# A first pass over an image batch: two rows a partition and one queue, against four rows, quarter tiles of the array and two queues

## The reference, cut to what matters

```python
# layer 0
d = conv(x, w_down, stride 2, pad 1, groups of 2 channels)   # 8 x 256 x 64 x 64
gate = f(k-means of the channels of d[0], a Gaussian mixture on their means)
y = bilinear_up_x2(repeat(gate * d + d, 2) * w_up) + x
# layer 1
xP = y (as 8 x 512 x 16384) @ P          # 64 low cosine products of row and column
out = gamma * attention(xP, Wq, Wk, Wv) + y
```

## Time and profile before

| | us |
|---|---|
| median of 3 runs | 2952.55 |
| lowest and highest | 2927.55 and 2962.68 |
| the profiled execution | 2949.2 |
| its span, first to last instruction | 2947.4 |

### The profile page before, as it was taken

One profiled execution on the slowest core, in us unless ns is written; L12 is line 12 of the kernel. 1 busy time (PEld: TensorE's weight loads), 2 busy tenths in 40 slices (PEclk: granted clock), 3 DMA queues, 4 the chain that ended last, 5 costly groups with the idle time before them and its releaser, 6 DMA issues.

```text
span 2947.4 us, 46132 instructions
## 1 busy us (share of the span) xinstructions
PE 2531.7 (86%) x17638; PEld 1666.6 (57%) x17638; DVE 2141.5 (73%) x2317; ACT 1185.5 (40%) x3193; POOL 1040.4 (35%) x772
## 2 busy tenths in 40 slices
PE   8999999999999666378499989888888887888887
PEld 2233223233323164044389888878778887788776
DVE  3777767677766743165499998988788888888886
ACT  0000000000000020033377777767666676766764
POOL 5444444444444000000044444444434343343433
PEclk9999999999999875689699999999999999999998
DMA  9999999999999660630499999999999999999998
GB/s 318 305 313 307 298 303 316 298 300 309 309 298 304 193 281 18 187 38 0 177 357 416 416 415 402 406 390 380 384 370 386 371 389 374 385 361 376 375 379 326
DMA packets 622924, 923.48 MB, mean 313 GB/s; under 512 B 208641, under 2 KB 471169, under 8 KB 620290
## 3 DMA queue, kind: packets, MB, share of 16 engines
q1 hardware_dynamic: 622722, 920.73, 90.1%
HBM read 615.00 MB, written 303.56 MB: 312 GB/s over the span
## 4 chain that ended last, share of the span: by engine, by line
DMA 33%; PE 11%; DVE 3%; ACT 2%; issue 2%; SPq 1%; POOL 0%; DVEq 0%
DMA out<-second_x 25%; PE second_o L1245 7%; DMA second_x<-in_x 4%; DMA second_dd<-downsampled 4%; DVE second_x L1469 1%; PE second_mid_t L1215 1%; DVE second_left L1018 1%; DVE second_mid L1450 1%; SPq L1051 1%; PE second_st L1105 1%; ACT second_mid L1334 1%; ACT second_left L1346 1%; POOL second_left L1018 0%; PE second_zt_t L1228 0%; ACT second_part L1334 0%
## 5 line engine op out<-in xcount | busy, mean ns | idle before, releaser
L1245 PE MATMUL second_o<-second_right,second_left 128*128 128x128 f32 x8192 | 1081.4, 281 | 110.9 <-issue 44.3
L1018 POOL TENSOR_TENSOR second_left<-second_mid_copy,second_coef_rep 64x1024 f32<-64x1024 f32 x256 | 608.6, 2377 | 1350.5 <-ACT second_mid_copy L1355 1329.5
L1245 PEld LDWEIGHTS second_o<-second_right,second_left 128*128 128x128 f32 x8192 | 999.3, 196 | 144.8 <-issue 134.7
L1469 DVE SCALAR_TENSOR_TENSOR second_x<-second_o,second_shift,second_x 128x512 f32<-128x512 f32 x1024 | 735.3, 738 | 222.9 <-PE second_o L1245 118.3
L278 PE MATMUL first_conv<-first_x,first_band 128*64 128x512 f32 (+1 forms) x3072 | 735.6, 618 | 19.4 <-POOL first_band L213 11.2
L278 PEld LDWEIGHTS first_conv<-first_x,first_band 128*64 128x64 f32 x3072 | 238.3, 135 | 510.5 <-issue 460.5
L225 DVE TENSOR_TENSOR first_product<-first_freq,first_cols 128x4096 f32<-128x4096 f32 x64 | 283.2, 4424 | 310.5 <-PE first_freq L294 310.0
L206 POOL TENSOR_TENSOR first_band<-first_shift,first_w_all 128x576 f32<-128x576 f32 x256 | 289.6, 1152 | 541.1 <-PE first_conv L278 533.8
L260 ACT ACTIVATE first_staged<-first_conv 128x512 f32<-128x512 f32 x128 | 76.5, 597 | 923.5 <-PE first_conv L278 923.5
L1334 ACT ACTIVATE second_mid<-second_dd,all_inter 128x128 f32<-128x128 f32 x1024 | 313.3, 388 | 85.8 <-DMA second_dd<-downsampled 83.6
L1334 ACT ACTIVATE second_part<-second_dd,all_inter 128x128 f32<-128x128 f32 x1024 | 313.2, 388 | 3.2
(11 more groups left out here) (219 smaller groups left out, 1415.9 us busy)
## 6 DMA issues: line engine op xcount, KB each, us to landing
first_x<-in_x SPq DMA_DIRECT2D x256, 1024.0 KB, 11.0
second_x<-in_x SPq DMA_DIRECT2D x256, 1024.0 KB, 14.3
out<-second_x SPq DMA_DIRECT2D x256, 1024.0 KB, 16.4
downsampled<-first_staged SPq DMA_DIRECT2D x128, 256.0 KB, 8.6
gather_d<-downsampled SPq DMA_DIRECT2D x16, 2048.0 KB, 16.4
second_dd<-downsampled SPq DMA_DIRECT2D x64, 512.0 KB, 14.9
second_p<-in_p_cols SPq DMA_DIRECT2D x1, 4096.0 KB
gates_ft<-all_wv SPq DMA_DIRECT2D x64, 32.0 KB, 5.4
```

Of the source, the lines that this page charges most:

```text
L1018: return eng.tensor_tensor(left[a][rows, odd:HALF:2, :, :].rearrange("p n (t s) g -> p n t s g", t=T), turned[rows, :, :, :].unsqueeze(3). ...
L1245: last = nc.tensor.matmul(ob[n][:, r, :], left[a][:, r, n, :], right[a][:, r, :], start=True, stop=True)
L1469: nc.vector.scalar_tensor_tensor(out=xt[i][:, n // S, n % S, rows, :], in0=ob[n][:, :, :], scalar=shift[:, n:n + 1], in1=xt[i][:, n // S, ...
```

## The change

A tile now holds four channels on 128 partitions: 32 blocks of four adjacent rows each. A run is 2 KB, a load 2 MB in 1024 runs, a group two tiles, and the ring has 7 tiles (as many bytes as before). The band matrix has 3 x 6 blocks of 32 columns, one multiplication and no addition, on half as many tiles.

For the convolution a group's two tiles stand in the two column halves of the array, and the two halves of the partitions (two channels each) are separate products that go to two banks. For three of the row offsets the band is 64 rows by 64 columns (24 products of a group), for the boundary rows 64 rows by 32 columns (24 products). The whole group is convolved before ScalarE is told. `project` still has 16 products of 128 rows by 32 columns.

The stores leave SyncE. ScalarE issues them on its own queue: behind each copy it waits for that copy, and issues four transfers of 32 partitions (64 KB in runs of 256 B). What is stored, and where, is unchanged.

```diff
-    xv = x.rearrange("b (c s) (i r) w -> c (s i) b (r w)", s=S, r=2)
+    xv = x.rearrange("b (n q) (i r) w -> n (q i) b (r w)", q=2 * S, r=BLOCK1)
...
                 for g in range(GROUPS1):
-                    for pair in (2 * g, 2 * g + 1):
-                        store(pair)
-                    for unit in range(g * GROUP1 + SLOTS1, (g + 1) * GROUP1 + SLOTS1):
-                        if unit < UNITS1:
-                            load(unit)
+                    for tile in range(2 * g + SLOTS1, 2 * g + 2 + SLOTS1):
+                        if tile < TILES1:
+                            load(tile)
...
             def _(act):
                 for pair in range(pairs):
-                    act.wait_ge(conv_made, pair + 1)
+                    act.wait_ge(conv_made, pair // 2 + 1)
...
                     nc.scalar.activation(staged[pair % STAGED][:, :, :], conv_ps[pair % CONV_BANKS][:, :, :], ACT.Copy
                                          ).then_inc(conv_copied, 1)
+                    act.wait_ge(conv_copied, pair + 1)
+                    for a in range(2):
+                        for e in range(2):
+                            at = a * 64 + e * 32
+                            act.dma_start(xdv[pair // 2 * GROUP1 + 2 * a + pair % 2, e],
+                                          staged[pair % STAGED][at:at + 32, :, :]).then_inc(stored[pair % STAGED], 16)
...
+                    def product(r, n, width, place, dw, first, last):
                         left = 1 if dw < 0 else 0
                         at = dw + 2 * left
+                        for a in range(2):
+                            for k in range(2):
+                                tile, part = 2 * g + a, slice(k * 64, k * 64 + 64)
+                                made = nc.tensor.matmul(
+                                    conv_ps[(2 * g + k) % CONV_BANKS][a * HD + place:a * HD + place + width * BLOCKS1,
+                                                                      :, left:],
+                                    band[tile % WEIGHTS1][part, dw + 1, n:n + width, :].rearrange("p n i -> p (n i)"),
+                                    xt[tile % SLOTS1][part, :, r, at:at + 2 * (WD - left) - 1:2],
+                                    start=first, stop=last)
+                        return made
+
+                    for dw in (0, 1, -1):
+                        product(1, 0, 2, 0, dw, dw == 0, False)
+                        product(3, 2, 2, 0, dw, False, False)
+                    for dw in (0, 1, -1):
+                        product(0, 4, 1, 0, dw, False, dw < 0)
+                        made = product(2, 5, 1, BLOCKS1, dw, False, dw < 0)
+                    made.then_inc(conv_made, 1)
```

More of the change, by code:

```diff
@@ L99 @@
 GROUPS1 = UNITS1 // GROUP1
-SLOTS1 = 14
-WEIGHTS1 = 8
+BLOCK1 = 4
+BLOCKS1 = H // BLOCK1
+TILES1 = GROUPS1 * 2
+SLOTS1 = 7
+WEIGHTS1 = 4
+EDGES = [(1, (2, 0)), (3, (0, 2)), (0, (1,)), (2, (1,))]
+BANDS = [dh for _r, dhs in EDGES for dh in dhs]
 CONV_BANKS = 4
@@ L106 @@
 HALF_B = B // 2
-TAPS = [(0, 0), (1, 0), (0, 1), (1, 1), (0, -1), (1, -1)]
-FIRST_COLS = [("shift", 3 * HD), ("rows", S * 2 * 32), ("low_rows", 2 * 32), ("cols", LOW * W), ("low_cols", LOW * WD)]
+FIRST_COLS = [("shift", len(BANDS) * BLOCKS1), ("rows", BLOCK1 * 32), ("low_rows", 2 * 32), ("cols", LOW * W), ("low_cols", LOW * WD)]
 SLOTS = 4
 def first_pass(nc, x, w_rows, first_cols, xd, xp, xpd):
-    xv = x.rearrange("b (c s) (i r) w -> c (s i) b (r w)", s=S, r=2)
-    xdv = xd.rearrange("b t g (h w) -> (t g h) b w", w=WD)
+    xv = x.rearrange("b (n q) (i r) w -> n (q i) b (r w)", q=2 * S, r=BLOCK1)
+    xdv = xd.rearrange("b t g (i e w) -> (t g) e i b w", e=2, w=WD)
     xpv = xp.rearrange("(n m) b r c -> b m r n c", m=GROUP1)
     with Scope(nc, "first") as sc:
[L119 to L122, removed]
+        xt = [sc.sb(f"x{i}", [P, B, BLOCK1, W]) for i in range(SLOTS1)]
+        w_all = sc.sb("w_all", [P, TILES1, 3 * len(BANDS)])
+        band = [sc.sb(f"band{i}", [P, 3, len(BANDS), BLOCKS1]) for i in range(WEIGHTS1)]
+        shift, rows = sc.sb("shift", [P, len(BANDS), BLOCKS1]), sc.sb("rows", [P, BLOCK1, 32])
         low_rows = sc.sb("low_rows", [P, 2, 32])
@@ L133, in first_pass @@
         x_in = [sc.sem(f"x_in{i}") for i in range(SLOTS1)]
-        scaled, banded = sc.sem("scaled"), sc.sem("banded")
+        banded = sc.sem("banded")
         conv_made, conv_copied = sc.sem("conv_made"), sc.sem("conv_copied")
@@ L144, in _, with load @@
             def _(sp):
[L145 to L156, removed]
+                def load(tile):
+                    slot = tile % SLOTS1
+                    if tile >= SLOTS1:
+                        sp.wait_ge(freq_made, (tile - SLOTS1) // 2 + 1)
+                    sp.dma_start(xt[slot][:, :, :, :].rearrange("p b r w -> p b (r w)"), xv[tile]
+                                 ).then_inc(x_in[slot], 16)
                 def store_freq(first, last):
@@ L167, in _ @@
                 tiles = (shift[:, :, :].rearrange("p a b -> p (a b)"),
-                         rows[:, :, :, :].rearrange("p a b c -> p (a b c)"),
+                         rows[:, :, :].rearrange("p a b -> p (a b)"),
                          low_rows[:, :, :].rearrange("p a b -> p (a b)"),
@@ L175, in _ @@
                 sp.dma_start(w_all[:, :, :].rearrange("p c k -> p (c k)"), w_rows).then_inc(const_in, 16)
-                for unit in range(SLOTS1):
-                    load(unit)
-                    if unit == 1:
+                for tile in range(SLOTS1):
+                    load(tile)
+                    if tile == 1:
                         for n in (3, 4):
@@ L193, in _ @@
                 for i in range(STAGED):
-                    sp.wait_ge(stored[i], len(range(i, pairs, STAGED)) * 16)
+                    sp.wait_ge(stored[i], len(range(i, pairs, STAGED)) * 64)
                 sp.wait_ge(freq_out, 2 * 2 * GROUP1 * 16)
@@ L200, in _ @@
                 pool.wait_ge(const_in, 64)
[L201 to L213, removed]
+                shape = [P, 3, len(BANDS), BLOCKS1]
+                for tile in range(TILES1):
+                    if tile >= WEIGHTS1:
+                        pool.wait_ge(conv_made, (tile - WEIGHTS1) // 2 + 1)
+                    nc.gpsimd.tensor_tensor(
+                        band[tile % WEIGHTS1][:, :, :, :], shift[:, :, :].unsqueeze(1).broadcast_to(shape),
+                        w_all[:, tile, :].rearrange("p (a b) -> p a b", a=3).unsqueeze(3).broadcast_to(shape),
+                        ALU.mult).then_inc(banded, 1)
             @block.vector
@@ L255, in _ @@
                 for pair in range(pairs):
-                    act.wait_ge(conv_made, pair + 1)
+                    act.wait_ge(conv_made, pair // 2 + 1)
                     if pair >= STAGED:
-                        act.wait_ge(stored[pair % STAGED], pair // STAGED * 16)
+                        act.wait_ge(stored[pair % STAGED], pair // STAGED * 64)
                         act.wait_ge(low_made, (pair - STAGED) // (2 * SPAN) + 1)
@@ L261, in _, with convolve @@
                                          ).then_inc(conv_copied, 1)
+                    act.wait_ge(conv_copied, pair + 1)
[4 more added lines that the diff above has]
+                                          staged[pair % STAGED][at:at + 32, :, :]).then_inc(stored[pair % STAGED], 16)
             @block.tensor
             def _(pe):
[L265 to L271, removed]
+                def convolve(g):
+                    if g >= CONV_BANKS // 2:
+                        pe.wait_ge(conv_copied, 2 * (g - CONV_BANKS // 2) + 2)
+                    pe.wait_ge(banded, 2 * g + 2)
+                    for tile in (2 * g, 2 * g + 1):
+                        pe.wait_ge(x_in[tile % SLOTS1], (tile // SLOTS1 + 1) * 16)
+                    def product(r, n, width, place, dw, first, last):
@@ L272, in convolve @@
                         left = 1 if dw < 0 else 0
                         at = dw + 2 * left
[L274 to L281, removed]
@@ L282, in convolve @@
-                    last.then_inc(conv_made, 1)
+                        for a in range(2):
[7 more added lines that the diff above has]
+                                    start=first, stop=last)
@@ L288, in project @@
                         pe.wait_ge(freq_taken, g - FREQ_BANKS + 1)
-                    for n in range(4):
-                        j, r = n // 2, n % 2
+                    for r in range(BLOCK1):
                         for q in range(4):
[L292 to L296, removed]
+                            half, a = q // 2, q % 2
+                            last = nc.tensor.matmul(
+                                bank[32 * q:32 * q + 32, :, :], rows[:, r, :],
+                                xt[(2 * g + a) % SLOTS1][:, half * HALF_B:(half + 1) * HALF_B, r, :],
+                                start=r == 0, stop=r == BLOCK1 - 1)
                     last.then_inc(freq_made, 1)
@@ L311, in _ @@
```

(13 more changed lines are left out.)

## The result

The changed kernel takes 2759.45 us, median of 4 runs (2754.47 to 2764.88), against 2948.60 for the kernel before: a ratio of 0.9364, with a 95% interval of 0.9304 to 0.9425. The profiled execution took 2754.47 us with a span of 2752.7.

The account below looks back on a forecast made before the run. Transfers and TensorE, nearly equal in price, were taken to bound the first pass. 62 periods less 1.64 us (15.44 to 13.8), plus 2.8 at the end, take 104 us off 2949.2: 2845 us, range 2764 to 2950.

Parts of the forecast that it names:

- the stores: First pass, a group's 0.524 MB of stores in 256 B runs: 2.9 us, bounds 2.3 and 3.49.
- the transfers after: First pass, a group's loads and stores after the change: 13.8 us, bounds 12.3 and 15.44.
- the second rival: First pass: transfers gain more (loads 10.0, stores 2.3 to 2.5 us), TensorE's 12.3 bounds, period 12.5, 2764 us; chance 0.07.
- the loads: First pass, a group's 4.194 MB in 2 KB runs: 384 GB/s, 10.92 us, bounds 11.95 and 10.0.
- TensorE: First pass, TensorE's work a group after the change: 12.3 us, under the transfers, if row halves work beside each other.
- ScalarE: First pass, two copies of 0.60 us and eight issues of 0.52 a group: 5.4 us, hidden below the period.
- The last rival's other half: First pass: ScalarE held 2.95 us at each issue, 24.8 us a group, 3530 us; decides from 1.78 us; chance 0.04.
- The third rival: First pass: ScalarE's issues stand behind SyncE's loads and exclude each other, period 16.3, 3000 us; chance 0.07.
- The quarter stores: First pass, eight 64 KB transfers a group in place of two of 256 KB: up to 4.13 us.
- The estimate of 7.6 us for eight: First pass, by the skill's 0.95 us for a 64 KB transfer: eight cost 7.6 us, period 18.5, 3140 us.

Follow-up runs that it names:

- e4: Changed kernel without 16 of a group's 24 small products, stores on ScalarE's queue: 2758.82 us, period 12.40 us.
- e6: Kernel before without its two left taps (8 of 24 products of a group), stores on SyncE's queue: 2937.66 us, period 15.42 us.
- e7: Kernel before without its two left taps, each 256 KB store issued by ScalarE on its own queue: 2808.27 us, period 13.12 us.
- e9: Kernel before without its two left taps, stores on SyncE's queue but issued after the next group's loads: 2930.92 us, period 15.36 us.
- e8: Changed kernel with both row halves of each product read from partitions 0 to 63: 3305.8 us, period 20.67 us.
- e10: Kernel before without its two left taps, ScalarE's stores cut into four of 32 partitions (64 KB each): 2793.61 us, period 13.12 us.
- e5: Changed kernel without 16 of a group's 24 small products, stores on SyncE's queue: 2992.59 us, period 15.99 us.
- e2: Kernel before with ScalarE issuing each 256 KB store on its own queue, all else as before: 2917.45 us, 0.987 of the kernel before.
- e1: Changed kernel with its eight 64 KB stores a group issued by SyncE again, ahead of the loads: 2996.19 us, 1.013 of the kernel before.
- e13: Changed kernel without 16 of a group's 24 small products, each 2 MB load cut into two by images: 2745.43 us, period 12.30 us.
- e3: Changed kernel with each load cut by row pairs into two of 1 MB, runs of 1 KB: 2903.08 us, 0.9802 of the kernel before.

## Why the prediction was wrong

**The term that failed: the stores.** The forecast gave them 2.9 us a group, bounds 2.3 to 3.49, both from the kernel before, where they stand in line with the loads on SyncE's queue, and carried the price over to ScalarE's. The step "the transfers after" moved the stores to another queue and counted no effect of it. Measured against the loads' own 11.95 us (1 KB) they cost 15.42 - 11.95 = 3.47 us in line and 13.12 - 11.95 = 1.17 on their own queue. In the changed kernel the loads alone ran at 392 and 387 GB/s:

```profile
15.00:20.00 5.00, 0.54 (x4) 0.33 (x8) 0.00 (x0) 0.00 (x0) 0.00 (x0) 1.00 1.05 392
20.00:25.00 5.00, 5.00 (x35) 1.56 (x31) 0.00 (x0) 0.00 (x0) 0.00 (x0) 1.00 1.05 387
```

At 388 they are 10.8 us a group, and the stores 12.40 - 10.8 = 1.6. That 1.6 is an upper end, as e4's 12.40 is; the bytes alone are 1.35. The forecast's lower bound was at least 0.7 too high. Its upper one, 3.49, was the true price before: e6 has 3.47 with transfers as the only bound. The idle time that I read from the share of 1.02 beside 1.10 was there, but it belonged to that price. A 256 B packet takes 18 ns in e6 as in e7, which is 2.3 us a group on 16 engines, and most of the rest is the engines standing behind the stores (e9 above; in e6 at least 6.7% of their time, 1.0 us a group). On a queue of their own that is gone. With at most 1.6 for 2.9 the transfers need at most 12.4, and TensorE's 12.5 is the bound: 62 x 2.95 + 2.8 = 186 us, the 185.5 of the profile. That the time is the second rival's 2764 is in part luck: TensorE was its bound too, but it had the loads at 10.0 and the stores at 2.3 to 2.5.

**Right: the loads.** The line through 1 KB and 4 KB put 2 KB at 384 GB/s; 387 to 392 were measured. The trace of before could have said so: against the prediction's "no run of 2 KB" it holds 768 packets of 2048 B between 1420 and 1445 us, in a later stage, at 85.3 ns each by their own lengths, the line's figure.

**Right: TensorE.** 12.3 us was forecast, 12.49 measured; the convolution is 8.49 for 8.26. Row halves stand beside each other, as column parts do, and e8 shows it by taking it away. The Trainium skill's rule that different tiles load and multiply in parallel (TensorEngine Tiling (Array Packing), Key Properties) agrees with the trace: four products of 64 x 64 go in a step of 0.45 us.

**Right in sign, wrong in size: ScalarE.** An issue was to take 0.52 us, because little stands on its queue. The tile's answer gives minimum, median and maximum in ns, after and then in e10:

```profile
L258 ACTq DMA_DIRECT2D downsampled<-first_staged x512: 309/1430/3295, 30.5 to 820.6; - x171
```

```profile
L262 ACTq DMA_DIRECT2D downsampled<-first_staged x476: 309/474/1544, 20.3 to 797.2; - x159
```

In e10, beside 1 KB runs, the median is 0.47, in the changed kernel 1.43. The mean there, from 200 to 700 us, is 1.28: eight issues and two copies come to 8 x 1.28 + 1.2 = 11.4 us a group, and with the short steps between them ScalarE waits for TensorE in only some 24 of these 500 us. It stayed hidden, since TensorE's waits for ScalarE sum to 6.7 us by the weight loads, but there is little room left. The last rival's other half, ScalarE held at each issue, thus has its mechanism in the trace, at 1.28 us, under the 1.78 from which the forecast let it decide. The third rival has not: ScalarE is at its issues for 407 of these 500 us and SyncE for 385, so they don't exclude each other.

**The quarter stores.** They were to cost up to 4.13 us a group. The cut costs nothing on ScalarE's queue (e10). On SyncE's, where the forecast didn't look, the eight stores cost 15.99 - 10.8 = 5.2 (e5). The estimate of 7.6 us for eight is far above both.

**The chance.** The case that came, TensorE as the bound, had 0.07, since I let the stores fall to no less than 2.3. The bounds of an unseen cost were worked out in the old place of the operation; an estimate for the new place is the bytes alone, 0.524 MB at the loads' 388 GB/s, 1.35 us (no bound: in e7 the stores cost 1.17, where their bytes at 351 GB/s are 1.49). With that, transfers could have fallen under TensorE's 12.3, and the range's lower end would have been 2949 - 62 x 3.14 - 2.8 = 2752.

**What each part is worth.** The queue alone brings 1.3% (e2), as TensorE's 15.0 is next. The other parts without the queue lose 1.3% (e1). Both are less than the 2% below which the forecast would tell no difference, but their intervals leave out 1, and the periods, 14.95 and 16.20 against 15.44, say the same. Together they bring 6.4%: transfers and TensorE were nearly equal before, 15.4 and 15.0, and are again, 12.1 to 12.4 and 12.5, with VectorE at 11.1 and ScalarE at 11.4 just beside them. None of the runs pointed to a version that beats the changed kernel by more than runs differ; e13's 2745 leaves products out.

## What to carry to other kernels

When an operation is moved to another queue, its price must be worked out in the new place: the price that it had in line with others was here only a bound from above, and its bytes at the stream's rate were near what it then cost (1.35 against at most 1.6). When two resources bound a stage at nearly equal price, shorten one on purpose (leave work out) and read the other's floor; here that took four single runs and showed what the time of the whole kernel could not show.

## What the runs showed of the hardware that was not expected

- A queue that carries both 1 KB loads and stores in 256 B runs moved 306 GB/s; with the stores on a second queue the same 16 engines moved 358 (e6, e7). In line, a group's 2048 short runs cost 3.47 us, beside the loads 1.17, though a packet of 256 B took 18 ns in both; in line the engines stood partly empty behind the stores, with loads already issued (share 0.63 in e9).
- On SyncE's queue, eight stores of 64 KB between loads of 2 KB runs cost 5.2 us a group (e5), two of 256 KB between loads of 1 KB runs 3.5 (e6). On ScalarE's queue eight or two made no difference (13.12 in both, e7 and e10). Why the cut costs in the one place alone stays open.
- ScalarE was held at an issue for 0.47 us beside 1 KB loads (e10) and 1.43 beside 2 KB loads (after), by the medians. The run's size alone isn't the cause: with 2 KB loads and a transfer share of 0.73 it was 0.48 (e8), and with loads cut to 1 KB in the changed kernel 0.56 (e3).
